# Linear attention and output product from high and low parts, in a two-layer network on one core

## The reference, cut to what matters

```python
x = _ln(x, ln1_w, ln1_b)
qk = _silu(x @ Wqk.T + bqk)                      # 64 columns
v = _silu(x @ Wv.T + bv)                         # 512 columns
heads = qk[..., None, :] * gamma + beta          # four heads of 64
quad_q, lin_q, quad_k, lin_k = map(_rope, heads)
attn = relu(quad_q . quad_k / 64 + bias) ** 2    # inside groups of 64 tokens
lin_kv = sum over tokens(lin_k x v) / n          # 64 x 512 per batch
out = gate * (attn . v + lin_q . lin_kv)         # gate = silu(x @ Wg.T + bg)
return _ln(out @ Wo.T + bo, ln2_w, ln2_b)        # Wo: 512 -> 256
```

## Time and profile before

| | us |
|---|---|
| median of 3 runs | 1087.06 |
| lowest and highest | 1086.01, 1089.81 |
| the profiled execution | 1088.44 |
| its span, first to last instruction | 1086.8 |

### The profile page before, as it was taken

How to read it: one execution, slowest core, us unless ns; L and a number is a source line. 1 busy time by engine, 2 the same in 40 slices (tenths; PEclk the granted TensorE clock), 3 DMA queues, 4 the chain that set the end, 5 groups by cost and what they waited for, 6 DMA issues and landing times.

```text
span 1086.8 us, 20552 instructions
## 1 busy us (share of the span) xinstructions
PE 1044.9 (96%) x6154; PEld 896.6 (83%) x6154; DVE 798.4 (73%) x1842; ACT 393.8 (36%) x794; POOL 432.9 (40%) x408
## 2 busy tenths in 40 slices
PE   5999999999999999989999999999999999999995
PEld 4899888888989798967868788888888888867774
DVE  5667987798788877786866777777777777763745
ACT  2544454445443536352410222232323232352300
POOL 2723666566656565254112110101001000088886
PEclk7999999999999999989999999999999999999998
DMA  8333344544454436331055556424355151265556
GB/s 253 106 114 120 128 163 140 187 147 141 147 176 145 143 113 226 106 101 50 6 159 171 189 179 210 155 97 148 113 180 195 56 197 50 75 140 86 75 101 146
DMA packets 87255, 147.69 MB, mean 136 GB/s; under 512 B 8433, under 2 KB 64625, under 8 KB 87025
## 3 DMA queue, kind: packets, MB, share of 16 engines
q1 hardware_dynamic: 66416, 98.11, 27.8%
q0 software_dynamic: 20736, 48.28, 16.2%
HBM read 88.91 MB, written 57.45 MB: 135 GB/s over the span
## 4 chain that ended last, share of the span: by engine, by line
PE 68%; DVE 14%; POOL 6%; issue 6%; DMA 4%; ACT 1%; DVEq 0%; POOLq 0%; SPq 0%; ACTq 0%
PE wide L2072 19%; PE wide L592 11%; PE bank L592 11%; PE bank L2072 9%; PE wide L1553 3%; PE bank L2097 3%; POOL first_half L1485 3%; DVE hT L1022 2%; PE wide L1646 2%; DMA x_second<-slot_results_scratch,result_rows 2%; POOL x1b L1485 2%; PE bank L2065 1%; PE bank L1622 1%; POOL x_second L1485 1%; PE bank L1553 1%
## 5 line engine op out<-in xcount | busy, mean ns | idle before, releaser
L2130 ACT ACTIVATE gsT<-bank 128x512 fp32r<-128x512 f32 x71 | 42.5, 599 | 243.4 <-PE bank L2097 243.4
L1945 POOL DMA_DIRECT2D expert_ring<-experts_scratch x24 | 17.1, 711 | 253.3 <-DVE slots_h L2179 186.1
L2072 PEld LDWEIGHTS wide<-expert_ring,gsT 128*128 128x128 f32 x852 | 112.1, 189 | 6.6 <-issue 0.3
L2072 PE MATMUL wide<-expert_ring,xsT 128*128 x432 | 115.9, 404 | 0.9 <-DVE xsT L2161 0.8
L2072 PE MATMUL wide<-expert_ring,gsT 128*128 x852 | 114.0, 282 | 0.1
L2072 PE MATMUL bank<-expert_ring,xsT 128*128 x420 | 112.8, 403 | 0.5 <-issue 0.5
L2072 PEld LDWEIGHTS wide<-expert_ring,xsT 128*128 128x128 f32 x432 | 76.1, 188 | 15.1 <-issue 1.8
L563 POOL TENSOR_TENSOR folded_matrix<-fold,folded_matrix 128x512 fp32r<-128x512 f32 x48 | 64.5, 1350 | 59.7 <-ACT folded_matrix L778 59.6
L576 POOL DMA_INDIRECT slot_rows_scratch<-u,slot x64 | 66.5, 1039 | 49.9 <-issue 20.6
L2072 PEld LDWEIGHTS bank<-expert_ring,xsT 128*128 128x128 f32 x420 | 74.0, 188 | 14.1 <-issue 1.1
L592 PE MATMUL bank<-w,hT 128*128 128x264 f32 x480 | 61.5, 285 | 0.5 <-DVE hT L1022 0.5
(11 more groups left out here) (322 smaller groups left out, 2481.9 us busy)
## 6 DMA issues: line engine op xcount, KB each, us to landing
experts_scratch<-folded_matrix SPq DMA_DIRECT2D x24, 1024.0 KB, 5.2
expert_ring<-experts_scratch POOLq DMA_DIRECT2D x24, 1024.0 KB, 5.5
raw<-in_expert_weights SPq DMA_DIRECT2D x24, 512.0 KB, 6.2
xs_ring<-slot_rows_scratch SPq DMA_DIRECT2D x71, 128.5 KB, 2.5
slot_results_scratch<-ys_ring SPq DMA_DIRECT2D x71, 128.0 KB, 2.6
lora<-in_expert_lora SPq DMA_DIRECT2D x24, 288.0 KB, 3.2
u<-in_L_attn_x SPq DMA_DIRECT2D x4, 1024.0 KB, 5.5
expert_bias<-in_expert_bias POOLq DMA_DIRECT2D x8, 512.0 KB, 6.9
```

What stands on the lines that cost most here:

```text
L2072: ins = mm(o, parts[i], moving, start=(first and q == 0), stop=(last and q == 2))
L2130: return nc.scalar.activation(o, i, ACT.Copy)
```

## The change: operands of the linear part and of the output product split in two

1. `YY`: `oT` and `wo1` become two float32r parts each. The product is twelve float32r matmuls of 256 columns instead of four float32 ones. `wo1` is loaded raw and split once (`WH:3` on ACT, `WL:3` on DVE). `OO` on DVE now writes a ring `og` of three slots; ACT copies it to the high part (`OH:n`, 16 in a half); the low part is a subtraction (`OL:n`), on POOL in the first half and on DVE in the second.
2. The linear part of `OO`: `lkT` holds the keys twice, so `LK` gives lin_kv in both halves of its rows. ACT copies all 128 rows as high part, DVE replaces rows 0 to 63 by the low part (`LK` on DVE). lin_q is split too (`QH` on ACT, `QL` on DVE, 4 each in a half); its high part stands twice. Two float32r matmuls of 512 columns (128 rows, and 64 rows) replace one float32 matmul.
3. `q` and `r` have one buffer each instead of two, so `QK:n` on ACT waits for `HB:n-1`.
4. The lists of all stages are written anew: both attention halves, and also layer 0's turn, the mixed stretch and `AHEAD`. In the second half's start `XB:0` is first on DVE and moves in front of the last expert tiles; `LX:1` on SP is issued two to three tiles earlier.
5. Small things: some loads share a semaphore; the load of `wo1` waits for layer 0's hidden parts to be read; the first expert rows wait for `AT:3` and `KT:3` instead of `HB:3`.

```diff
@@ tensor, attention
                 if e == 0:
                     pe.wait_ge(v_ready, T0 + TPB * b + TPB)
                     pe.wait_ge(*g_free(("LK", b)))
+                    pe.wait_ge(q_ready, H0 + h + 1)
                     pe.wait_ge(att_ready, H0 + h + 1)
-                mm(o, lkv[:, e * P:(e + 1) * P], headA[:, h % 2 * 512:(h % 2 + 1) * 512], start=True, stop=False)
+                mm(o, lkv[:, of], q_parts[:, at], start=True, stop=False)
+                mm(o, lkv[QK:, of], q_low[QK:, at], start=False, stop=False)
...
                 if n % 4 == 0:
-                    for e in range(EC):
-                        pe.wait_ge(*g_free(("OO", EC * h + e)))
+                    pe.wait_ge(o_ready, O0 + EC * h + EC)
                 for e in range(EC):
-                    last = mm(o[:, 0:DIM], oT[:, h % 2, e, n % 4 * P:(n % 4 + 1) * P], wo1[:, e, :], start=(e == 0),
-                              stop=(e == EC - 1))
+                    last = times(o[:, 0:DIM], lambda i: oT[:, i, e, n % 4 * P:(n % 4 + 1) * P], lambda i: wo1[i][:, e, :],
+                                 e == 0, e == EC - 1)
@@ scalar, attention
-                copy(lkv[QK:, :], g_full(act, un)[QK:, :], 1.0 / SEQ).then_inc(g_free(un)[0], 1)
+                copy(lkv[:], g_full(act, un), 1.0 / SEQ).then_inc(kv_high, 1)
+            elif kind == "QH":
+                copy(q_parts[QK:, at], headA[QK:, at]).then_inc(q_high, 1)
+            elif kind == "OH":
+                act.wait_ge(*g_free(("OO", n)))
+                if n >= EC and n % EC == 0:
+                    act.wait_ge(*g_finished(("YY", n - 1)))
+                copy(oT[:, 0, n % EC, :], og[:, n % GATES, :]).then_inc(o_high, 1)
@@ gpsimd, first half
+            elif kind == "OL":
+                pool.wait_ge(o_high, O0 + n + 1)
+                nc.gpsimd.tensor_tensor(oT[:, 1, n % EC, :], og[:, n % GATES, :], oT[:, 0, n % EC, :], ALU.subtract
+                                        ).then_inc(o_ready, 1)
@@ vector, attention
             elif kind == "OO":
+                if n >= GATES:
+                    hold(dve, v_held, o_ready, O0 + n - GATES + 1)
                 dve.wait_ge(*g_free(("GA", n)))
-                tt(oT[:, h % 2, e, :], g_full(dve, un), gT[:, n % GATED, :], ALU.mult).then_inc(g_free(un)[0], 1)
+                tt(og[:, n % GATES, :], g_full(dve, un), gT[:, n % GATED, :], ALU.mult).then_inc(g_free(un)[0], 1)
+            elif kind == "LK":
+                dve.wait_ge(kv_high, B0 + n + 1)
+                stt(out=lkv[0:QK, :], in0=g_full(dve, un)[0:QK, :], scalar=1.0 / SEQ, in1=lkv[0:QK, :], op0=ALU.mult,
+                    op1=ALU.subtract).then_inc(g_free(un)[0], 1)
@@ lists that the prediction speaks of (new)
layer 0, tensor:  AV:0+ W1:0+ TP:1+ EP:2+ LT:0+ W1:1+ W1:2+ TP:2+ AV:1+ EP:3+ CN:0 S:4+ W1:3+ LT:1+ VV:6+ VV:7+ FC:0+
   (before)       ... CN:0 S:4+ VV:6+ AV:1+ VV:7+ FC:0+, and the next turn begins LT:1 W1:4 W1:5
layer 0, vector:  ... EP:2+ CH:0 SA:0+ LT:0+ W1:0+ W1:1+ AV:1+ EP:3+ CH:1 VV:6+ ...
   (before)       ... TP:1+ SA:0+ CH:0 EP:2+ F1:0 W1:0+ LT:0+ W1:1+ EP:3+ CH:1 AV:1+ VV:6+ ...
first half, tensor:  ... GA:4 LK:0 GA:5 OO:0 GA:6 OO:1 ... OO:12 OO:13 YY:8 YY:9 YY:10 YY:11 OO:14 GA:15 OO:15 YY:12 YY:13 YY:14 YY:15
   (before)          ... GA:15 YY:9 OO:12 OO:13 OO:14 YY:10 OO:15 YY:11 YY:12 YY:13 YY:14 YY:15
second half, tensor: ... GA:13 GA:14 GA:15 OO:12 YY:8 OO:13 OO:14 OO:15 YY:9 YY:10 YY:11 YY:12 ...
second half, gpsimd: ... GZ1:11 YS:9 GZ1:12 GZ0:14 GZ0:15 GZ1:13 YS:11 GZ1:14 GX1:13 GZ1:15 YS:13 GX1:14 GX1:15 YS:15
AHEAD, experts to second half, vector: "MA:64:1 MC:70:1 MO:69:1", sync: "MT:62:1 MT:63:1" (before: "MO:69:1" and "")
```

More of the change, by code:

```diff
@@ L42 @@
 GATED = 4
+GATES = 3
 ROUND = 6
@@ L162, in build @@
         keep = {
-            "held": {e: sem(f"{e}_held") for e in ("tensor", "vector", "gpsimd")},
+            "held": {e: sem(f"{e}_held") for e in ("vector", "gpsimd")},
             "ident": sb("ident", [P, P]),
@@ L217, in tile_rooms @@
     keep["v"] = a.take("v1", [P, TPB, H1])
-    keep["lkT"], keep["lkv"] = a.take("lkT", [P, TPB, P]), a.take("lkv", [P, H1])
+    keep["lkT"], keep["lkv"] = a.take("lkT", [P, TPB, P]), a.take("lkv", [P, H1], F32R)
     keep["att"], keep["attw"] = a.take("att", [P, TPB, P]), a.take("attw", [P, 2, 4, P])
@@ L533, in factors @@
             pool.sem_inc(factors_ready, 1)
-        nc.gpsimd.memset(half[:], -0.5).then_inc(half_ready, 1)
-        pool.wait_ge(half_ready, 1)
+        own(nc.gpsimd.memset(half[:], -0.5))
         def unit(u):
@@ L1686, in unit @@
                     copy(u[:, b, t % TPB, 0:DIM], u[:, b, t % TPB, 0:DIM], keep["r2"][:, at:at + 1]).then_inc(u_ready, 1)
+            elif kind == "WH" and n == 3:
+                act.wait_ge(keep["late_in"], 64)
+                copy(wo1[0][:], keep["wo1_raw"][:]).then_inc(w_high, 1)
             elif kind == "WH":
@@ L1752, in unit @@
                 last.then_inc(spread_ready, 1)
+            elif kind == "WL" and n == 3:
+                dve.wait_ge(w_high, n + 1)
+                tt(wo1[1][:], keep["wo1_raw"][:], wo1[0][:], ALU.subtract).then_inc(w_split, 1)
             elif kind == "WL":
@@ L2004, in unit @@
                     scattered(sp)
-                    sp.wait_ge(*before["heads_done"])
+                    for read in before["heads_done"]:
+                        sp.wait_ge(*read)
                     sp.wait_ge(keep["ranks_ready"], 4)
```

299 lines of the change are left out of this document (163 added, 136 removed).

## The result

The changed kernel took 1108.88 us (median of 4 runs, 1108.51 to 1109.72) beside 1087.58 us for the kernel before (4 runs, 1086.01 to 1089.81) on the same chip: ratio 1.0195, 95% interval 1.0176 to 1.0215. It is slower by about 2%; the forecast was 1.1% faster. The profiled execution of the changed kernel took 1108.51 us, its span is 1106.8.

A forecast was written before the change was run, and what follows sets the result against it. PE was taken as the limit, joined by an equally full POOL in the second half. Layer 0 -5, transition -1, first half -6.2 + 1.0, experts +0.3, second half -0.7 sum to -11.6: 1075.5 us from 1087.06, range 1065 to 1085.

The forecast's parts named there:

- PE is the only limit there, so the 11.2 us arrive: First attention half: PE's 11.2 us of saved work shorten it, less the longer way from OO to YY.
- The linear pair at 0.46 us, bound 0.12 to 0.23 a product: Linear part of OO: two float32r products take 0.46 instead of 0.86 us, saving 6.4 us of PE in each half.
- Stall of 3.3 us at YY:12 in the first half, with 1.5 us of slow clock: First half's end: no cover from OO:15 to YY:12, so PE stalls 3.3 us, then 1.5 us of slow clock.
- The other covers between OO and YY: First half: enough PE work between OO:3, OO:7, OO:11 and YY:0, YY:4, YY:8 to make the 3.0 us hand-over free.
- Collisions, a third of 16 and 1.0 us on PE: First half: a third of POOL's 16 subtractions collide with DVE's work, costing PE +1.0 us; ends 0 and +8.
- B: Rival: POOL's subtractions hold DVE, PE stalls 8 us more, second half waits 3 us; 1086.5 us, no change; chance 0.12.
- C: Rival: OO-to-YY hand-over stalls at about three of seven other places, layer 0 gives nothing; 1097 us, slower; chance 0.06.
- Second half -0.7: Second half, held by POOL: -1.5 earlier start, +1.3 wait for YY:9, -0.5 at the end; sum -0.7 us.
- The earlier start of POOL: Second half's start: with XB:0 out of the way POOL starts about 1.5 us sooner.
- Experts +0.3: Experts, lists at their borders only: XB:0 costs DVE 2.28 us among tiles, +0.3 us; ends 0 and 2.3.
- Layer 0 -5: Layer 0's new list: LT:1's wait for AV:1 (4.6 us in three batches) goes; -5 us, ends -13 and +3.
- Transition -1: Turn from layer 0 into the first half: same heads built by DVE before KT:1; -1 us, ends -7 and +4.

The follow-up runs named there:

- 128 rows: Changed kernel with the second linear product over 128 rows instead of 64: 1107.75 us with one tile for the low part, 1109.89 us with two.
- the other order: Changed kernel with the end of the second half's PE and DVE lists reordered, products standing between YY:11 and YY:12: 1110.64 us, ratio 1.0047 to the kernel before.
- two pairs of runs: SP queue at the experts' start as before, MT:0 ahead of SX:3: on the changed kernel 1107.66 us; with both splits undone 1101.13 us, beside 1103.95 without it.

## Why the prediction was wrong, step by step

- **"PE is the only limit there, so the 11.2 us arrive"** is the step that failed. In its place the runs showed a half that grew by 8.0 us: PE's work fell by 3.7 us only, PE idled 8.3 us and lost 3.4 to a slow clock. The earlier trace rows shows a first half with no idle PE, and I took that as 31 us of spare room on DVE. But many of DVE's steps stand in a chain with PE on both sides, and then it counts when each ends, not their sum. Even where all 11 us of PE work were gone (128 rows), the half took 112.0 us: 11.7 idle and some 5 of slow clock.
- **The linear pair at 0.46 us, bound 0.12 to 0.23 a product**: measured 0.40 + 0.42, outside the bounds. Of the 11.2 us of each half, 6.4 were this term, and the unit of 1.74 us gave none of it. Rows of 128-row products alone could not bound it from above, because the price is of changing row count. The runs with 128 rows show it: 0.23 + 0.23. Those runs also show that the size of this term alone does not explain the time.
- **YY 1.43 us**: right. **Stall of 3.3 us at YY:12 in the first half, with 1.5 us of slow clock**: right (2.9 us, and half clock behind it). The other covers between OO and YY held too: no other YY of that half waited. The three further waits of 1.0 to 2.4 us stood where I had counted nothing, before two OO units and a gate product.
- **Collisions, a third of 16 and 1.0 us on PE**: nine DVE steps lost 8.9 us. One collision cost 0.7 to 1.2 us and not the 1.8 of the earlier trace rows, where the DVE step begins beside an indirect DMA of POOL (476.31 to 477.33) and then meets the operation at 477.34; but nine met, and two of the waits follow such steps. With the low parts on DVE the half was longer still (117.0), so the collisions are not the whole of it.
- **The rivals.** B, at 0.12, named DVE as held by POOL, but put 8 us of stalls on top of the 3.3 already in the sum and no slow clock; measured are 8.3 us in all, and it still counted on the 11.2 us of saved work. C, at 0.06, had the sign, and YY:12 of the second half is one of its seven other places; it wanted three of them, and left out the queue.
- **Second half -0.7**: +4.3 (-2.4 + 7.7 - 1.0). I did not see this in the diff: with one buffer for two parts, OH:12 waits for YY:11. I had counted "nothing" as cover between OO:15 and YY:12, but for the first half only, and took PE's idle time in the second as hidden under POOL. It was 8.3 us, POOL waits behind it, and the other order gave 3.3 of the 7.7 us back. The earlier start of POOL was right: the gap before it fell from 5.7 to 3.3 us, and it is released by the last store. Why the gathers still take 132 us in place of 128.5 stays open; POOL's waits for its own DMAs are 3.0 us with the other order and 1.8 in the kernel before.
- **Experts +0.3**: +10.2. I read the lists of PE and DVE at the border and left out SP's, though it was in the diff: 4.4 to 6.2 us by two pairs of runs. XB:0 is a wait of 1.1 us. About 2 us are work moved: three more PE units of the second half stand here, and the gap to POOL is 2.4 us shorter. The other 2 to 3 us stay open.
- **Layer 0 -5**: +1.7 on the first chip. LT's waits for DVE (4.6 us) went, and new ones of 1.9 us a batch before the hidden products came. **Transition -1**: -4.3 against the first profile and -0.8 against the second one; the long collision of the earlier trace rows is gone.
- Sum of the stages: +1.7 - 4.3 + 8.0 + 10.2 - 2.4 + 7.7 - 1.0 = 19.9 of the 20.0 us of span.

## What to carry to other kernels

Work taken off a full engine shortens a stage only if the operands come sooner too: count for each wait what the new steps in front of it add, also where they stand before other products than the changed ones. An engine that is busy for 70% of a stage can still hold it up, if its steps stand between two products. When one buffer takes the place of two, look for the wait that this adds at the end of the stage. Read each queue's list at a border, the DMA queue's above all, and ask what every transfer now stands behind.

## What the runs showed of the hardware

- A 64-row product between 128-row ones: the load unit idles 0.24 us before its weight load and again before the next one, and the pair's starts are 0.40 and 0.42 us apart. With 128 rows throughout they are 0.23 and 0.23 apart, and a unit takes 1.36 us in place of 1.74. Eight 64-row loads in a row took 0.96 us.
- DVE steps with operands in SBUF alone took 1.1 to 1.9 us instead of 0.4 to 0.8 where they ran beside a POOL instruction, in nine cases of the changed kernel's first half.
- In the changed kernel's first half the waits of 2.4 and 2.9 us were followed by a granted clock of 0.50, those of 1.9 and 1.0 us by 1.00; this took 3.4 us. The same waits of 2.9, 1.1 and 0.8 us, with the linear split undone, took 3.4, 1.7 and 0 us of slow clock in three runs on three chips. A wait of 1.9 us in layer 0 was followed by hidden products 0.12 us apart at full clock on the first chip and 0.22 apart at half clock on chip C, in the same kernel. So the length of a wait did not tell whether the clock fell.
- The kernel before took 1087 us on three chips and 1107 on three others. In its two profiles, one of either kind, the stages from layer 0's end on are equal within 3 us, so the difference lies in layer 0 there. The ratio of the two kernels was 1.0195 on one chip and 1.0061 on another. A ratio from one chip needs the chip's own base beside it.
